# 64-wide heads: the products with the values stand between a step's scores and its turned blocks

## The reference

```python
def _forward(x, Wq, Wk, Wv, Wo, qA, qB, kA, kB, vA, vB, oA, oB):   # NQ, NKV, HD, RANK = 16, 4, 64, 8
    b, s, _ = x.shape
    q = _lora_proj(x, Wq, qA, qB).reshape(b, s, NQ, HD).transpose(0, 2, 1, 3)
    k = _lora_proj(x, Wk, kA, kB).reshape(b, s, NKV, HD).transpose(0, 2, 1, 3)
    v = _lora_proj(x, Wv, vA, vB).reshape(b, s, NKV, HD).transpose(0, 2, 1, 3)
    ...
    q = _rope(q, cos_h, sin_h)
    k = _rope(k, cos_h, sin_h)
    k, v = jnp.repeat(k, 4, axis=1), jnp.repeat(v, 4, axis=1)
    attn = jax.nn.softmax(jnp.einsum('bhqd,bhkd->bhqk', q, k) * ATTN_SCALE, axis=-1)
    out = jnp.einsum('bhqk,bhkd->bhqd', attn, v)
    ...
    return _lora_proj(out, Wo, oA, oB)
```

## Time and profile before

| | us |
|---|---|
| median of 3 runs | 2696.03 (2695.88 to 2704.38) |
| the profiled execution | 2702.17 |
| its span | 2700.5 |
| TensorE busy, share of the span | 2166.2, 80% |
| VectorE | 1623.1, 60% |
| ScalarE | 1441.8, 53% |
| POOL | 795.0, 29% |
| mean granted clock of TensorE | 0.885 of full speed |

### The profile page before, as it was taken

The page is one execution under the profiler, slowest core; times in us unless marked ns, Lnnn a source line. Parts: engine busy times, 40 slices in busy tenths (PEclk is TensorE's granted clock), DMA queues, the critical chain, the costliest instruction groups (busy, mean ns, idle before and its releaser), DMA issues. The chain is left out here.

```text
span 2700.5 us, 37135 instructions
## 1 busy us (share of the span) xinstructions
PE 2166.2 (80%) x13682; PEld 1266.4 (47%) x13692; DVE 1623.1 (60%) x3485; ACT 1441.8 (53%) x2110; POOL 795.0 (29%) x432
## 2 busy tenths in 40 slices
PE   5999999999999356698266776999789236999798
PEld 3666666666666226233224342444357122444357
DVE  5978778778775566011565546677324775677324
ACT  3777777777775522687512353555542322555541
POOL 3877777777784011321012021000000121000000
PEclk7999999999999668799578896999989566999899
DMA  1000000000000400430401303110010003110010
GB/s 69 1 5 1 3 5 1 3 5 1 3 1 1 160 0 5 113 69 3 160 1 44 85 11 84 44 37 19 1 32 1 0 13 82 43 37 19 1 32 16
DMA packets 41707, 81.91 MB, mean 30 GB/s; under 512 B 10792, under 2 KB 19064, under 8 KB 37368
## 3 DMA queue, kind: packets, MB, share of 16 engines
q1 hardware_dynamic: 41528, 79.54, 10.7%
HBM read 65.14 MB, written 13.63 MB: 29 GB/s over the span
## 5 line engine op out<-in xcount | busy, mean ns | idle before, releaser
L692 ACT ACTIVATE probs<-psum_banks 128x1024 f32<-128x1024 f32 (+3 forms) x608 | 474.2, 826 | 363.5 <-PE psum_banks L557 256.6
L765 DVE TENSOR_REDUCE neg_max<-psum_banks 128x1 f32<-128x512 f32 (+3 forms) x672 | 398.6, 658 | 200.4 <-PE psum_banks L590 148.8
L1117 POOL TENSOR_SCALAR l0a_rows<-l0a_rows,l0a_rinv 128x1024 f32<-128x1024 f32 x160 | 454.4, 2845 | 189.0 <-DVE l0a_rinv L1079 185.4
L1067 DVE TENSOR_REDUCE l0a_nmax<-psum_banks 128x1 f32<-128x1024 f32 x256 | 312.5, 1221 | 137.8 <-PE psum_banks L961 136.0
L552 PE MATMUL psum_banks<-q_stack,k_stack 75*128 75x512 bf16 (+7 forms) x1216 | 323.1, 344 | 74.4 <-ACT probs L692 25.7
L1013 ACT ACTIVATE l0a_rows<-psum_banks,l0a_nmax 128x1024 f32<-128x1024 f32 x256 | 286.0, 1117 | 61.4 <-DVE l0a_nmax L1067 60.1
L586 PE MATMUL psum_banks<-k_stack,q_stack 72*128 72x128 bf16 (+3 forms) x1024 | 249.2, 326 | 78.6 <-DMA q_stack<-q_parts 66.4
L975 PE MATMUL psum_banks<-packed,l0a_rows 128*128 128x128 f32 x2048 | 267.1, 273 | 2.7 <-POOL l0a_rows L1117 1.6
L975 PEld LDWEIGHTS psum_banks<-packed,l0a_rows 128*128 128x128 f32 x2048 | 239.1, 141 | 42.9 <-issue 5.4
L960 PE MATMUL psum_banks<-l0a_kh,l0a_qw 128*128 128x512 f32 x512 | 242.1, 473 | 18.7 <-POOL l0a_qw L1106 13.0
L574 PE MATMUL psum_banks<-probs,v_ones 128*32 128x512 f32 (+3 forms) x2432 | 243.6, 516 | 7.5 <-ACT o_sum L661 6.5
(11 more groups left out here) (277 smaller groups left out, 3462.9 us busy)
## 6 DMA issues: line engine op xcount, KB each, us to landing
q_stack<-q_parts SPq DMA_DIRECT2D x96, 192.0 KB
k_stack<-k_parts SPq DMA_DIRECT2D x72, 192.0 KB
qkv<-in_l0f_w SPq DMA_DIRECT2D x6, 1024.0 KB, 5.3
q_parts<-parts SPq DMA_DIRECT2D x24, 256.0 KB, 3.3
k_parts<-parts SPq DMA_DIRECT2D x24, 256.0 KB, 4.2
moe_b<-in_l0f_b SPq DMA_DIRECT2D x32, 128.0 KB, 3.8
l1f_w<-in_l1f_w SPq DMA_DIRECT2D x16, 256.0 KB, 5.0
moe_w<-in_l0f_w SPq DMA_DIRECT2D x2, 1024.0 KB, 5.4
```

The source lines that it names most:

```text
L692: act.activation(S.Pt[:, U % PBUFS, 2 * half:2 * half + 2, c0:HALF], PS[:, bank:bank + 2, c0:HALF], ACT.Exp).then_inc(exp_done, 1)
L765: dve.tensor_reduce(out, scores, AX, ALU.max, negate=True).then_inc(job_read, 1)
L1067: dve.tensor_reduce(R.nmax4[:, s % 4:s % 4 + 1], scores(s), AX, ALU.max, negate=True).then_inc(max_done, 1)
L1117: rows_divided.mark(pool.tensor_scalar(R.Pr[:, s % RING, :], R.Pr[:, s % RING, :], R.rinv4[:, s % 4:s % 4 + 1], None, ALU.mult))
```

## The change

TensorE's order in a step is changed: the loop that issues the products (L978 to L990 before) stands ahead of the turned blocks. Its text, its waits and what it signals are the same, and no other engine's code is changed.

```diff
                     m.then_inc(rows_ready, 1)
                 t = s - NT - LATE
+                for v in (t - 2, t - 1) if 0 < t <= total and t % 2 == 0 else ():
+                    ps, kt = divmod(v, NT)
+                    pe.wait_ge(act_copied, v + 1)
+                    pe.wait_ge(dve_copied, v + 1)
+                    if v % STEPS == 0:
+                        pe.wait_ge(job_read, number["value", v // STEPS] + 1)
+                    if kt == 0 and ps >= 1:
+                        pe.wait_ge(o_read, ps)
+                    for a in range(2):
+                        m = pe.matmul(PS[HD * a:HD * (a + 1), 6, :], R.V[:, v // STEPS % B, kt, :],
+                                      (R.Pc, R.Pd)[v // 2 % 2][:, v % 2, a, :], start=kt == 0,
+                                      stop=kt == NT - 1, skip_group_check=True)
+                    m.then_inc(pv_done, 1)
                 if 0 <= t < total:
                     ps, kt = divmod(t, NT)
...
                         m.then_inc(turned, 1)
-                for v in (t - 2, t - 1) if 0 < t <= total and t % 2 == 0 else ():
-                    ps, kt = divmod(v, NT)
-                    pe.wait_ge(act_copied, v + 1)
-                    pe.wait_ge(dve_copied, v + 1)
...
-                    m.then_inc(pv_done, 1)
                 for job in at.get(s, ()):
                     spare(job)
```

## The result

The changed kernel takes 2797.3 us (median of 4 runs, 2791.30 to 2802.04) against 2695.95 before (median of 4). The ratio, which isn't the quotient of the two medians, is 1.0369, 95% interval 1.0344 to 1.0394. The forecast was 2798. The profiled execution took 2796.75 us, 94.6 more than that of before. The stage carries more than all of it: its last output product starts at 985.00 us instead of 883.38, 101.6 later; what follows took 7 us less in this execution, and its busy times are alike. That part runs the same code in every kernel of this document, and over the traces it takes 1810 to 1820 us from the start of the last output job on. So a few us of any difference in the whole time can come from it.

The account below looks back on a forecast made before the run. TensorE was taken to bound the wide_heads stage. Order 4.9, waits 21.5, 21.7 and 45.0, and clock 9 sum to 102 us; 2702.2 + 102 = 2804, less 6.1: 2798 us, range 2750 to 2842.

Parts of the forecast that it names:

- TensorE bounds the stage: In wide_heads TensorE is busy 99.54 of 100 us, so whatever makes it wait is lost.
- Edges: TensorE's block order without waits: a pair of steps takes 5.71 instead of 5.67 us, times 122, 4.9 us more.
- Term A: Pairs with rope parts, no extra job, not ending a group: products' second half waits 0.58 for VectorE's copy; 37 pairs, 21.5 us.
- ScalarE ... just hidden: ScalarE's exponential of the even scores ends near 2.44 us, due at 2.66: 0.2 in hand.
- Term B: Pairs with rope parts and an extra job: the job waits for the parts on bank 7, 0.70; 31 pairs, 21.7 us.
- Term C: Ends of groups of eight, 30 times: products wait for ScalarE's copy of bank 6; 51.0 less 6.0, net 45.0 us.
- Term D: TensorE's clock falls behind half of 11 gaps of 2.3 to 2.6 us, slowing the work behind: 9 us.
- The sum: All parts in wide_heads together: 4.9 + 21.5 + 21.7 + 45.0 + 9 = 102 us more.
- The check beforehand: Bank 6 reckoning: today's 13 waits are just the 13 group ends without an extra job, 0.46 us each.
- The faster rival: Turned blocks' loads hide under the products and bank 6's 6.0 us goes: 2671 us; chance 0.03.

Follow-up runs that it names:

- e3: Changed kernel with ScalarE's copy of finished bank 6 at the head of its step and VectorE's rope parts on odd steps; 2686.69 us.
- e2: Changed kernel with VectorE's rope parts moved from even to odd steps; 2723.60 us.
- e4: Kernel before, old order, with ScalarE's copy of finished bank 6 at the head of its step; 2692.49 us.
- e1: Changed kernel with ScalarE's copy of finished bank 6 moved to the head of its step; 2741.74 us.
- e8: Changed kernel with bank 6 copied first, rope parts on odd steps, and high and low parts six steps behind their job instead of five; 2687.05 us.
- e7: Kernel before, old order, with bank 6 copied first and rope parts on odd steps; 2706.35 us.
- e6: Kernel before, with products ahead of the turned blocks only in steps s = 4 mod 8; 2745.17 us.
- e9: Kernel before, old order, with bank 6 copied first, rope parts on odd steps, and high and low parts six steps behind their job; 2708.07 us.

## Why the prediction was right, step by step

- **TensorE bounds the stage, so each wait is lost:** shown by e3. With nearly all waits gone the changed order is as fast as the old.
- **Edges, +4.9 us:** wrong in sign. Scores ahead of products take 1.09 (345.01 to 346.10 above), not 1.18: they are 0.08 longer there than ahead of turned blocks, not the 0.17 that I carried over from turned blocks. Pairs without waits take 5.63, so -0.04 instead of +0.04: -5 us.
- **Term A, 0.58 in 37 pairs:** 6.29 - 5.63 = 0.66, since the products stood 0.10 earlier. With the edge it is +23.0 us; 21.5 and its edges 1.5 were forecast, the same. The mechanism holds as told in 29 of the pairs. For the other 8 the step that failed is "ScalarE ... just hidden": the prediction followed ScalarE only to its exponential and left out the division and the high part behind it, which make its odd copy late by itself (e2, products at 5.26 behind T(e)). In the kernel after, both copies end within 0.1 us of each other there, so for these pairs the number came out by luck.
- **Term B, 0.70 in 31 pairs:** the plain comparison gives +19.6, but before 10 of these pairs held a wait for bank 6. Against e4, which hasn't these waits, e1 has 0.69, 0.50 and 0.70 for rope, lora and value jobs, 20 us in all (22.9 with the edges forecast). Lora's 0.50 lies below the 0.58 even without the 0.12 for an exposed load; why isn't followed up.
- **Term C, 51.0 less 6.0:** the products came 6.41, 5.16, 6.45 (parts and job) and 6.02 (high part) behind T(e); forecast 6.41, 5.16, 6.41, 6.14. The 30 ends cost 61.5 us, of which 9.5 are the slower clock in the products behind, so 52. The waits of before, by e4, were 6.8.
- **Term D, 9 us:** the products behind the 10 gaps of 2.58 us took 2.31 to 3.56 instead of 1.87 in nine of ten, 9.5 us more; in the pairs that follow another 5 (B pairs of after less those of e1). 14 in all: larger, since the clock fell behind nine of the 11 gaps (nine of the ten of 2.58, and not behind the one of 2.20), not half, and the pair behind it pays too.
- **The sum:** 23.0 + 20 + 52 - 6.8 + 14, less 1 for the edges of the other pairs, is 101; the stage is 101.6 longer, the forecast said 102. The edges were off by -10, and the clock (+5), term A's wait (+3) and term C's (+2) by about as much the other way. So the waits were right to a few us, but that the sum meets the stage within 1 us and the forecast the median within 1 us is luck; the four runs alone span 11 us. The check beforehand, that the same chain gives today's 13 waits, speaks for term C alone.

In the changed kernel the turned blocks' loads start with their matmul behind the products (348.64 against 348.65 above), as in the trace before (868.09 both). So the pull of weight loads that the Trainium skill describes (page "TensorE: Matmul & The Clock Gate", Part 2) doesn't show across this edge. The page ties it to conditions, row groups that don't conflict or a background buffer for the weights, and no run here tests these. The faster rival's mechanism didn't appear, though the edge was shorter for another reason.

Among the variants e3 beats both kernels, by 9.6 us on before and 110.6 on after; e4 is 3.8 below before, and its interval overlaps with e3's, so which of the two is better isn't shown. In the traces the stage itself doesn't favour e3: from the second products to the 122nd it takes 761.2 us, e4 760.1, e8 756.0. What the new order gains on the old is thus the 4 us between e8 and e4, the shorter edges.

## What to carry to other kernels

On an in-order engine that is full, the time between a result and its next consumer is cover that other engines live on. Before moving a block, anchor a clock at each result that moves, walk each engine's queue in its own order to the next consumer, and count how many steps of the schedule have which extra work in that queue. Walk to the end of each queue: the one engine that I followed only halfway, ScalarE, was late by itself in eight pairs. The same move cost 101 us with the other engines' work where it was (before to after), 49 with bank 6's copy first (e4 to e1), and gained 18 with both moves (e7 to e3, each against its own runs of before). The extra work's best place depended on the order too: moving the rope parts gained 55 us in the new order (e1 to e3) and cost 12 in the old one (e4 to e7).

## What the runs showed of the hardware

- A single idle gap of 2.58 us, with dense work on both sides, lost TensorE's full clock in nine of ten cases (the granted clock of 280 to 283 us above is 0.67). In e2, gaps of 2.2 us lost it once in four, and the one such gap in the kernel after didn't; the 30 gaps of 1.3 to 1.4 in after, e2 and e6 never did. I had put the chance at a half. The length of the gap alone doesn't decide it: in e9 the clock fell behind the gap of 0.79 us at 170.74 (granted clock 0.52 in 171 to 174.5 us, and the products behind took 2.96 us instead of 1.87).
- A block of full-width float32r matmuls ahead of half-width ones took 0.08 us longer than ahead of full-width transposes (1.09 against 1.01), a block of transposes 0.17 longer ahead of products than ahead of scores (0.96 against 0.79). What makes the difference isn't settled.
